# Interleaving 28 fp32 transposes of a batch with the feed-forward's fp16 matmuls in a linear cross-attention kernel

## What is computed

```python
qh = einsum('bcn,oc->bon', layernorm(x), Wq)     # 8 heads of 64
kh, vh = (einsum('bcn,oc->bon', ctx, W) for W in (Wk, Wv))
qh = softmax(qh, axis=-2) * SCALE                # over the 64 of a head
kh = softmax(kh, axis=-1)                        # over the positions
context = einsum('bhdn,bhen->bhde', kh, vh)
out = einsum('bhde,bhdn->bhen', context, qh)
out = Wo @ out + bo
x = x + out / max(norm(out, axis=1), 1e-12) * g * sqrt(128)
x = x + einsum('bsi,io->bso', layernorm(x), dequant(qweight, scales, zeros)) + bias
```

## Time and profile before

| | |
|---|---|
| median of 3 runs | 750.89 us (750.7 to 751.72) |
| profiled execution: span from first to last instruction | 750.2 us |
| its own time | not listed apart from its span; the median of the runs is 0.7 us above the span |
| PE matmul busy | 713.0 us (95% of the span), 3895 instructions |
| PE weight loads (PEld) | 509.6 us (68%) |
| DVE busy | 611.3 us (81%) |
| ACT busy | 442.3 us (59%) |
| POOL busy | 399.8 us (53%) |
| mean granted TensorE clock | 0.983 of full speed |

### The profile page before, as it was taken

The page is one execution under the profiler, slowest core; times in us unless marked ns, Lnnn a source line. Parts: engine busy times, 40 slices in busy tenths (PEclk is TensorE's granted clock), DMA queues, the critical chain, the costliest instruction groups (busy, mean ns, idle before and its releaser), DMA issues.

```text
span 750.2 us, 12239 instructions
## 1 busy us (share of the span) xinstructions
PE 713.0 (95%) x3895; PEld 509.6 (68%) x3895; DVE 611.3 (81%) x1041; ACT 442.3 (59%) x756; POOL 399.8 (53%) x362
## 2 busy tenths in 40 slices
PE   4879899999999999999999999999999999999776
PEld 3646767677777767677777768677676777777442
DVE  4878879898888989888898888889898988888532
ACT  3766666574666657475656747565665647575311
POOL 3251645738374574738366563837557372843542
PEclk9979999999999999999999999999999999999996
DMA  8001020301102030200203030020303020010100
GB/s 304 5 29 57 3 82 0 114 1 55 59 29 84 0 112 0 91 21 28 84 0 112 0 112 0 31 81 3 108 0 112 0 65 19 0 57 1 56 21 36
DMA packets 12022, 37.00 MB, mean 49 GB/s; under 512 B 1480, under 2 KB 3040, under 8 KB 12000
## 3 DMA queue, kind: packets, MB, share of 16 engines
q1 hardware_dynamic: 12000, 36.72, 14.3%
HBM read 28.32 MB, written 8.39 MB: 49 GB/s over the span
## 4 chain that ended last, share of the span: by engine, by line
PE 82%; DVE 6%; issue 5%; ACT 4%; POOL 1%; DMA 1%; POOLq 0%; SPq 0%; DVEq 0%; ACTq 0%
PE ps_m L844 12%; PE ps_tb L817 7%; PE ps_m L890 6%; PE ps_m L891 6%; PE ps_k L788 4%; PE ps_k L789 4%; PE ps_k L790 4%; PE ps_o L788 4%; PE ps_o L790 4%; PE ps_tb L830 4%; PE ps_q L788 4%; PE ps_o L789 4%; PE ps_q L789 4%; PE ps_q L790 3%; PE ps_ta L830 3%
## 5 line engine op out<-in xcount | busy, mean ns | idle before, releaser
L358 POOL TENSOR_TENSOR q_exp<-q_exp,q_rec 128x512 f32<-128x512 f32 x128 | 142.1, 1115 | 303.9 <-DVE q_rec L626 302.8
L463 ACT ACTIVATE q_exp<-q_exp 128x512 f32<-128x512 f32 x128 | 80.6, 630 | 79.9 <-DVE q_exp L617 76.6
L631 DVE TENSOR_TENSOR q_lo<-ps_tb,q_hi 128x512 fp32r<-128x512 f32 x128 | 88.2, 689 | 47.3 <-ACT q_hi L470 46.7
L844 PE MATMUL ps_m<-k_t,c_t 128*128 128x512 f32 x256 | 115.3, 593 | 0.9 <-ACT c_t L553 0.8
L470 ACT ACTIVATE q_hi<-ps_tb 128x512 fp32r<-128x512 f32 x128 | 76.7, 599 | 34.4 <-PE ps_tb L817 32.8
L890 PE MATMUL ps_m<-w_int,x_lo 128*128 128x512 f16 x240 | 93.2, 389 | 1.5 <-DVE x_lo L696 1.5
L458 ACT ACTIVATE k_exp<-ps_k,k_nmax 128x1024 f32<-128x1024 f32 x64 | 71.2, 1112 | 38.6 <-DVE k_nmax L605 37.9
L617 DVE TENSOR_TENSOR q_exp<-ps_q,q_nmax 128x512 f32<-128x512 f32 x128 | 88.5, 691 | 6.0
L891 PE MATMUL ps_m<-w_int,x_hi 128*128 128x512 f16 x240 | 92.5, 386 | 0.0
L623 DVE TENSOR_REDUCE q_sum<-q_exp 128x8 f32<-128x512 f32 x128 | 86.1, 673 | 1.6
L612 DVE TENSOR_REDUCE q_nmax<-ps_q 128x8 f32<-128x512 f32 x128 | 87.1, 680 | 0.1
(11 more groups left out here) (118 smaller groups left out, 1492.2 us busy)
## 6 DMA issues: line engine op xcount, KB each, us to landing
x_in<-in_x SPq DMA_DIRECT2D x16, 512.0 KB, 4.9
c_in<-in_ctx SPq DMA_DIRECT2D x16, 512.0 KB, 3.3
x_res<-in_x SPq DMA_DIRECT2D x16, 512.0 KB, 4.2
out_x<-y SPq DMA_DIRECT2D x15, 512.0 KB, 2.9
og<-in_L_ffn_qweight SPq DMA_DIRECT2D x1, 512.0 KB, 5.3
sq<-in_L_ffn_qweight SPq DMA_DIRECT2D x1, 512.0 KB, 6.2
x2b<-in_L_ffn_qweight SPq DMA_DIRECT2D x1, 512.0 KB, 7.0
x<-in_L_ffn_qweight SPq DMA_DIRECT2D x1, 512.0 KB, 8.7
```

What stands on the lines that cost most here:

```text
L358: nc.gpsimd.tensor_tensor(chunk, chunk, rec, ALU.mult).then_inc(qs_done, 1)
L631: nc.vector.tensor_tensor(q_lo[:, :, j * P:(j + 1) * P], ps_tb[:].rearrange("p (c t) -> p c t", c=HC), q_hi[:, :, j * P:(j + 1) * P].bitca ...
L844: last = nc.tensor.matmul(ps_m[:], c_t[:, t, :], k_t[:, t, :], start=(t == 0), stop=(t == TC - 1))
```

## The change

The transposes are split into single tiles, and in turns that have both a projection and a feed-forward (`both`) 28 of the 88 transposes of a turn are put one by one ahead of single feed-forward matmuls: in steps 4 and 5 both key sets (8 transposes each among 8 matmuls), in step 6 the four query transposes that stood at the step's end (among the first four of 6 matmuls), in step 7 the eight context transposes (among the first eight of 10 matmuls). The number of instructions, their operands and every semaphore's count stay the same, as do the programs of the other engines. A wait stands now ahead of the first tile of its set.

```diff
+                def transpose_k_tile(k, t, tq_before):
+
+                    if t == 0:
+                        pe.wait_ge(kexp_done, 4 * a + k // 2 + 1)
+                        if begun(8 * a + k - 1):
+                            pe.wait_ge(tk_moved, 8 * a + k - 1)
+                        if k % 2 and begun(tq_before):
+                            pe.wait_ge(qlo_done, tq_before)
+                    tok = (4 * (k % 2) + t) * P
+                    done = nc.tensor.transpose((ps_ta, ps_tb)[k % 2][:, t * P:(t + 1) * P],
+                                               k_exp[:, (k // 2) % 2, tok:tok + P], ident[:])
+                    if t == 3:
+                        done.then_inc(tk_ready, 1)
...
+                def feed_forward_and_k(k0, j):
+
+                    for t in range(4):
+                        transpose_k_tile(2 * (j - 2), t, 0)
+                        feed_forward_lo(0, k0 + t)
+                        transpose_k_tile(2 * (j - 2) + 1, t, 8 * a + j - 4)
+                        feed_forward_hi(0, k0 + t)
+
+                def feed_forward_and_q(j):
+
+                    for t in range(2):
+                        transpose_q_tile(a, j - 4, 2 * t)
+                        feed_forward_lo(1, t)
+                        transpose_q_tile(a, j - 4, 2 * t + 1)
+                        feed_forward_hi(1, t)
+                    feed_forward(1, 2, 3)
+
+                def feed_forward_and_c():
+
+                    for t in range(4):
+                        transpose_c_tile(2 * t)
+                        feed_forward_lo(1, 3 + t)
+                        transpose_c_tile(2 * t + 1)
+                        feed_forward_hi(1, 3 + t)
+                    feed_forward(1, 7, TC)
...
-                    if 2 <= j < 6 and do_a:
+                    both = do_a and do_f
+                    if 2 <= j < 6 and do_a and not (both and j >= 4):
...
                         transpose_k(2 * (j - 2), 0)
...
-                    if j == 4 and do_f:
-                        feed_forward(0, 0, 4)
-                    if j == 5 and do_f:
-                        feed_forward(0, 4, TC)
-                    if j in (4, 5) and do_a:
+                    if j in (4, 5) and both:
+                        feed_forward_and_k(4 * (j - 4), j)
+                    elif j in (4, 5) and do_f:
+                        feed_forward(0, 4 * (j - 4), 4 * (j - 4) + 4)
+                    elif j in (4, 5) and do_a:
                         transpose_k(2 * (j - 2) + 1, 8 * a + j - 4)
...
-                    if j == 6 and do_f:
+                    if j == 6 and both:
+                        feed_forward_and_q(j)
+                    elif j == 6 and do_f:
                         feed_forward(1, 0, 3)
...
-                    if j == 7 and do_f:
+                    if j == 7 and both:
+                        feed_forward_and_c()
+                    elif j == 7 and do_f:
                         feed_forward(1, 3, TC)
...
-                    if j >= 4 and do_a:
+                    if j >= 4 and do_a and not (both and j == 6):
                         transpose_q(a, j - 4)
```

More of the change, by code:

```diff
@@ L810, in project_q, with transpose_q_tile @@
                     three(ps_q[:], xn_hi[s][:, tc], xn_lo[s][:, tc], wq_hi[:], wq_lo[:]).then_inc(q_ready, 1)
+                def transpose_q_tile(b, j, fc):
+                    if fc == 0:
+                        pe.wait_ge(qs_done, 8 * b + j + 1)
+                        if begun(8 * b + j):
+                            pe.wait_ge(qlo_done, 8 * b + j)
+                    done = nc.tensor.transpose(ps_tb[:, fc * P:(fc + 1) * P],
+                                               q_exp[:, j, fc * P:(fc + 1) * P], ident[:])
+                    if fc == HC - 1:
+                        done.then_inc(tq_ready, 1)
@@ L812, in transpose_q @@
                 def transpose_q(b, j):
-                    pe.wait_ge(qs_done, 8 * b + j + 1)
-                    if begun(8 * b + j):
-                        pe.wait_ge(qlo_done, 8 * b + j)
                     for fc in range(HC):
-                        last = nc.tensor.transpose(ps_tb[:, fc * P:(fc + 1) * P],
-                                                   q_exp[:, j, fc * P:(fc + 1) * P], ident[:])
-                    last.then_inc(tq_ready, 1)
-                def transpose_k(k, tq_before):
[L823 to L827, removed]
+                        transpose_q_tile(b, j, fc)
@@ new lines, in transpose_c_tile @@
+                def transpose_c_tile(t):
+                    if t == 0:
+                        if isinstance(i, int) and i == 0:
+                            pe.wait_ge(vo_moved, 2)
+                        if do_c:
+                            pe.wait_ge(att_done, 2 * (c + 1))
+                    done = nc.tensor.transpose(ps_o[t // 4][:, (t % 4) * P:(t % 4 + 1) * P],
+                                               c_in[s][:, t * P:(t + 1) * P], ident[:])
+                    if t % 4 == 3:
+                        done.then_inc(tc_ready, 1)
@@ L828, in transpose_k @@
+                def transpose_k(k, tq_before):
                     for t in range(4):
[L829 to L832, removed]
+                        transpose_k_tile(k, t, tq_before)
                 def mix_m(t0, t1):
@@ L874, in mix_out, with feed_forward_lo @@
                         last.then_inc(out_ready, 1)
+                def feed_forward_lo(h, k):
+                    ps_y = ps_q if h == 1 and not do_a else ps_m
+                    if k == 0:
+                        if h == 0:
+                            if isinstance(i, int) and i == 2:
+                                pe.wait_ge(w_converted, 2 * RC)
+                            pe.wait_ge(x2hi_done, 2 * (f + 1))
+                            pe.wait_ge(x2lo_done, 2 * (f + 1))
+                            if do_c:
+                                pe.wait_ge(m_moved, c + 1)
+                        elif do_a:
+                            pe.wait_ge(ymul_done, 2 * f + 1)
+                    nc.tensor.matmul(ps_y[:], x2_lo[:, k, :], halves(w_int[:, k // RC, k % RC, :])[h],
+                                     start=(k == 0), stop=False)
@@ L876, in feed_forward, with feed_forward_hi @@
+                def feed_forward_hi(h, k):
+                    ps_y = ps_q if h == 1 and not do_a else ps_m
+                    done = nc.tensor.matmul(ps_y[:], x2_hi[:, k, :], halves(w_int[:, k // RC, k % RC, :])[h],
+                                            start=False, stop=(k == TC - 1))
+                    if k == TC - 1:
+                        done.then_inc(y_ready, 1)
                 def feed_forward(h, k0, k1):
-                    ps_y = ps_q if h == 1 and not do_a else ps_m
                     for k in range(k0, k1):
[L879 to L891, removed]
@@ L892, in feed_forward @@
-                    if k1 == TC:
-                        last.then_inc(y_ready, 1)
+                        feed_forward_lo(h, k)
+                        feed_forward_hi(h, k)
+                def feed_forward_and_k(k0, j):
[4 more added lines that the diff above has]
+                        feed_forward_hi(0, k0 + t)
@@ L959, in iteration @@
                                 last.then_inc(rb_ready, 1)
-                    if j == 7 and do_f:
+                    if j == 7 and both:
+                        feed_forward_and_c()
+                    elif j == 7 and do_f:
                         feed_forward(1, 3, TC)
[L962 to L973, removed]
+                    elif j == 7 and do_a:
+                        for t in range(TC):
+                            transpose_c_tile(t)
                     if 2 <= j < 6 and do_a:
```

1 line of the change is left out of this document (added).

## The result

The changed kernel takes 816.9 us (median of 4 runs, 816.65 to 817.92) against 750.8 in the runs taken with it: 1.087 times as long, 95% interval 1.0857 to 1.0891. It is slower, as forecast, but by 66 us instead of 43, and outside the range of 779 to 806.

What follows compares the result with a forecast made beforehand. TensorE's list was taken as the bound. Transposes at unchanged price plus waits of 3.07 us in each of 14 turns (43.0 us), on a span of 750.2 and 0.7 to the median, gave 793.9 us, range 779 to 806.

Steps and rivals of the forecast that it cites:

- What bounds the kernel: TensorE's list: a matmul under way all the time at full clock, 43.05 us a turn, so any wait opened is lost in full.
- part 1: Price of the 28 moved transposes between fp16 matmuls: 0.109 us each as in a group, so nothing gained or lost.
- Part 2, the waits: Banks asked for too early in steps 4, 5, 6, 7 and ahead of the sums of squares: 3.07 us a turn, 43.0 in all.
- the sum: Span of 750.2 plus 43.0 us of waits is 793.2; 0.7 more for the median of the runs gives 793.9 us.
- What stays covered: Delayed work of ScalarE, VectorE and GpSimd and the context load fit into idle time: costed at nothing.
- the 0.97 of step 6: Wait for `ps_tb` behind step 6's projection: reuse takes 2.14 us, asked for after 1.17, so 0.97 us a turn.
- rival (a): Clock falls to 1.2 GHz around the sums and step 6 wait, on top of the waits: 803 to 812 us; chance 0.14.
- the old turn: Evidence against a clock fall: before the change, as long a run of sums and transposes without a wait keeps 1.00.
- the 0.40 us ahead of them: Wait ahead of the sums of squares, for ScalarE's copy out of `ps_ta`: 1.05 - 0.65 = 0.40 us a turn.
- The rival's own worst case of 812: The clock falling in all of the turns, 18 us on top of the waits: 812 us, left out of the range.
- its milder half: The part of rival (a) taken into the range; falls in half of the turns were put at 9 us, 803 us.

Runs made afterwards that it cites:

- `late`: Changed kernel with 24 of the 28 transposes still interleaved, but only where their banks are free, so no wait is left: 752.3 us against 752.8 before the change.
- `halves`: Kernel before the change, with six context transposes cut to half the weight load and six of step 1's eight to half the moving columns: 756.2 us, one run.
- `both14`: Changed kernel plus one idle matmul in the wait ahead of the sums of squares and four in the step 6 wait: 796.4 us.
- `q_only`: Changed kernel with only step 6's query transposes still interleaved, steps 4, 5 and 7 as before the change: 769.1 us, against 751.2 before.
- `k_only`: Changed kernel with only the key transposes of steps 4 and 5 still interleaved, steps 6 and 7 as before the change: 783.3 us, against 751.2 before.
- `sums1`: Changed kernel plus one idle fp16 matmul in the wait ahead of the sums of squares: 816.6 us.
- `fill4`: Changed kernel plus four idle fp16 matmuls in the step 6 wait, behind the projection: 816.7 us.

## Why the prediction was partly wrong

*What bounds the kernel, and part 1:* right. Pairs take 0.32 us, `late` gains nothing, and `halves` shows that the load doesn't set a transpose's price.

*Part 2, the waits:* right in place, releaser and size: 0.64 in step 5, 0.97 in step 6, 0.4 in step 7, and 3.15 us in an undisturbed turn for 3.07. `both14` puts them at 45 us for the whole kernel, forecast 43. (The 0.7 us between span and time in the sum came from two different executions; one execution takes 1.9 us more than its own span, as 816.9 and 815.0 show. The forecast time, 43.0 on the median of before, doesn't depend on it.)

*What stays covered:* right in the whole change; VectorE's list binds step 7 when that part stands alone. The prediction's own terms give it: without the 0.97 of step 6 TensorE asks at 5.46 - 0.97 = 4.49, and the list allows 4.11 + 1.28 + 0.10 = 5.49, a wait of 1.0.

*The step that failed* is rival (a): the fall of the clock was given a chance of 0.14 and nothing in the sum. It came in 13 of 14 turns and makes some 20 us of the 66. Two reasons stood against it, and neither held. One was the projection of 0.71 us between the sums and the wait of step 6: it stands in the stretch ahead of the fall (652.20 to 655.50) and didn't prevent it. The other was the old turn, which keeps 1.00 with as long a run of sums. That run has no wait on either side, and the runs show that waits on one side are enough for falls. `q_only` has only the wait behind the sums and `k_only` only those ahead of them, and each falls in 3 of 13 steady turns. `sums1` fills the wait ahead and falls in 13 turns; `fill4` fills the one behind, and the clock is down before the fillers begin; only `both14`, with both filled, keeps 1.00. The rival named the wait behind the sums alone and left out the 0.40 us ahead of them.

The fall's price was too low as well: 1.3 us, from the norms and a projection of turn 1, where in the changed turn it comes over step 6's fp16 matmuls and costs 1.57 (3.31 for 1.74). The rival's own worst case of 812 was so 5 us short, and the range, which took in only its milder half, ended at 806.

*Open:* what exactly makes the clock fall in one turn and not in the next, why the changed kernel falls in 13 turns where a kernel with a part of its waits falls in 3 to 5, and why turns with a fall gather at 47.7 to 47.8 us. That two fillers remove what neither removes alone is shown; the condition behind it is not.

## What to carry to other kernels

Before a bank's next writer is moved forward in a list, count the round trip of the bank from its last writer through all its readers (here 2.1 us for 0.44 us of transposes) and what still covers it; on the engine that bounds the kernel every missing tenth is paid in every turn. Waits on TensorE next to work of few moving columns, as the sums of squares are, cost nearly half as much again through the clock here (20 us on 45), so a forecast with such waits should carry the fall in its sum. And before interleaving to hide a weight load, look at the spacing in a group and behind its last member: here both were 0.109 us, and nothing was hidden.

## What the runs showed of the hardware

- An fp32 transpose of a 128x128 tile takes 0.109 us, 0.06 with 64 moving columns, and still 0.11 with half the weight columns (`halves`). The Trainium skill, "TensorE: Matmul & The Clock Gate", section on LDWEIGHTS in Part 2, gives a load as its columns over 1.2 GHz, by estimate 107 ns for 128, which fits the 0.109 in size and not in cause; the measurement decides. The moving columns don't set every price, though: the sums of squares move one column each, and still start (1.84 - 0.25) / 15 = 0.11 us apart (16 of them in the earlier trace rows, a single one lasts 0.25). Whether their load sets that, no run here tests.
- Adding work can shorten a kernel: five idle matmuls a turn, all in waits, took the changed kernel from 816.9 to 796.4 us; its turns 2 to 14 keep the clock at 1.00 (`both14`).
- Idle time in a timeline row understates a wait on TensorE by about 0.16 us, the part of the record of the matmul ahead that runs on past its own 0.22 (0.38 us for an fp16 matmul of 512 columns).
